# One tanh over two neighbouring sums: 16 instructions of 4096 columns in place of 32 of 2048

## The chip, the cores and the metric

The kernel runs on one core of a Trainium2 chip. The metric is the time of one execution on the device in microseconds (us). Its engines are TensorE (PE in the rows; PEld is its weight load), VectorE (DVE), ScalarE (ACT), GpSimd (POOL) and SyncE (SP), which here only issues transfers. They run their own instruction lists in order and wait for each other by semaphores.

## The reference

The reference is a small decoder of four layers on 16 batches of 64 tokens with 128 features. Each layer adds a kind of attention and a mixture of experts to `x`. The change touches only the attention of layer 2:

```python
def _L2_xattn_ref(features, masks, textual_features, q_masks, Ws, W, w, b, Wcw, bcw, Wcb, bcb):
    txt_proj = jnp.einsum('btd,de->bte', textual_features, Ws)
    feat_proj = jnp.einsum('bfd,de->bfe', features, W)
    h = jnp.tanh(txt_proj[:, None, :, :] + feat_proj[:, :, None, :] + b[None, None, :, :][..., 0, :])
    rho = jnp.einsum('bftd,d->bft', h, w[:, 0])
    qm = q_masks.astype(jnp.float32)
    rho = rho + (1.0 - qm)[:, None, :] * NEG
    att = jax.nn.softmax(rho, axis=-1)
    txt_h = jnp.einsum('bft,btd->bfd', att, textual_features)
    w_s = jnp.tanh(jnp.einsum('bfd,od->bfo', txt_h, Wcw) + bcw)
    b_s = jnp.tanh(jnp.einsum('bfd,od->bfo', txt_h, Wcb) + bcb)
    return w_s * features + b_s
```

For each batch, each of 64 feature rows is summed with each of 64 text rows, 128 values each; tanh of all of it, and a product with the vector `w`.

## The kernel before

Everything is kept with the 128 features on partitions and the 1024 tokens in the free dimension, in two halves `t` of 512. The stage before ends with a norm (`norm(4)`) and the next begins with `norm_rest(5)` and the experts of layer 2. Between them stands `pair_sums`, once for each engine, with each engine's work written out by hand in one loop over `g`.

The work is cut into 32 couples `g` of a batch `g // 2` and one half of its feature rows, 32 rows by 64 text rows, so 2048 columns each. Couple `g` goes through these steps:

- its sum, `work<-...`, is made by VectorE for even `g` (L1151, `sumA`) and by GpSimd for odd `g` (L1471, `sumB`), into buffer `g % 6` of `pairs`, which lies in `work`;
- its tanh is taken in place by ScalarE (L858), with the bias `l2b` from a tile;
- its dot with `w` is made by TensorE (L571) in four products of 512 columns, into one of two PSUM banks (couples 0 to 15, then 16 to 31). When it is done, the buffer is free for the sum of `g + 6`.

Other work stands in the same loops at fixed couples, and its place decides who waits for whom:

- TensorE projects keys for layer 3 ahead of the dots of 4 and 5 (L426, L427), which VectorE rotates at `g` 7 and 8, ahead of sum 8 (L1017 to L1019). Then TensorE projects values ahead of each dot of 8 to 15 (L436), two steps for each of four parts, and VectorE copies a part at `g` 11, 13, 15 and 17 (L1035), so ahead of sums 12, 14, 16 and 18.
- VectorE makes the softmax of the first 16 couples at `g` 20 (L1095 to L1097); ScalarE's exponential for it stands at `g` 19 (L836). The shares and the weighing stand at 22 and 24, and ScalarE's small tanh of the weights at `g` 25 (L841).
- TensorE spreads these weights ahead of the dots of 28 and 29 (L546), and VectorE updates the first half of `x` at `g` 30, ahead of sum 30 (L1123 to L1126). Ahead of the dot of 31 TensorE makes the mean of the next norm (L372).

Behind the loop follow the softmax and the update of the second half, and the next norm.

Of the kernel before, what the change touches and what calls it, by code (L numbers as in the profile page):

```python
# [21 lines left out]
ACT = mybir.ActivationFunctionType  # L22
# [59 lines left out]
def flamingo(nc, a, out):  # L82
    ctx = ExitStack()
    with ctx:
# [3 lines left out]
        def sem(name):  # L88
            return ctx.enter_context(nc.semaphore(name))
# [42 lines left out]
        l2pad, l2uvpad, l2b = packed["l2pad"], packed["l2uv"], packed["l2b"]  # L132
# [40 lines left out]
        pairs = work[:, 0:12 * T].rearrange("p (r c) -> p r c", r=6)  # L173
# [32 lines left out]
        x2 = {k: sem(f"x2_{k}") for k in ("feat", "fb", "sumA", "sumB", "tanh", "dot", "soft", "exp", "wb", "tw", "d", "bc")}  # L206
# [24 lines left out]
        def half(t):  # L231
            return slice(t * HALF, (t + 1) * HALF)
# [21 lines left out]
        POOL_SUMS = [g for g in range(2 * B) if g % 2]  # L254
# [106 lines left out]
        def _(pe):  # L361
            def keep_busy(count, bank):


                for _ in range(count):
                    pe.matmul(ps[:, bank], ident16, warm, start=True, stop=True)

            def norm_mean(j, t):

                if j:  # L370
                    pe.wait_ge(x_done[t], j)
                pe.matmul(ps[:, t], cen_w, x[:, half(t)], start=True, stop=True).then_inc(ln["mean"], 1)  # L372

            def norm_var(j, t):

                pe.wait_ge(ln["sq"], 2 * j + t + 1)
                for i in range(HT):
                    c = t * HT + i
                    mm = pe.matmul(ps[:, 2 + t, i:i + 1], sq[:, c * P:(c + 1) * P], var_w[:, :], start=True, stop=True)  # L379
                mm.then_inc(ln["var"], 1)  # L380

            def norm_spread(j, t):

                pe.wait_ge(ln["diag"], 2 * j + t + 1)
                pe.matmul(ps[:, 4 + t], ones_w[:, :], diag[:, half(t)], start=True, stop=True).then_inc(ln["bc"], 1)  # L385
# [37 lines left out]
            def prepare_keys(i, t):  # L423

                w, bank = (wqk1, wqk3)[i], KBANK[i][t]
                pe.matmul(ps[:, bank], w[:, 2], ctxT[:, half(t)], start=True, stop=True)  # L426
                pe.matmul(ps[:, bank + 1], w[:, 3], ctxT[:, half(t)], start=True, stop=True).then_inc(pre["proj"], 1)  # L427

            def prepare_values(i, q, part=None):

                w, r = (wqk1, wqk3)[i], 4 * i + q
                if q >= 2 and not part:
                    pe.wait_ge(pre["vcp"], r - 1)
                for b in range(4 * q + 2 * (part or 0), 4 * q + (2 if part == 0 else 4)):
                    for h2 in range(2):
                        mm = pe.matmul(ps[h2 * S:(h2 + 1) * S, VBANK[i] + q % 2, (b % 4) * P:(b % 4 + 1) * P],  # L436
                                       ctxT[:, b * S:(b + 1) * S], w[:, 4], start=True, stop=True)
                if part != 0:
                    mm.then_inc(pre["v"], 1)
# [103 lines left out]
            def weights_out(t, r):  # L543

                pe.wait_ge(x2["d"], 2 * t + r + 1)
                pe.matmul(ps[:, (0, 6)[t] + r], ones_w[:, :], (diag, sq)[r][:, half(t)], start=True, stop=True).then_inc(x2["bc"], 1)  # L546

            def pair_sums():

                pe.wait_ge(pre["txtcp"], 2)  # L550
                for t in range(2):
                    pe.wait_ge(ln["n"], 2 * 4 + t + 1)
                    pe.matmul(ps[:, FEAT[t]], l2w[:, 1], n[:, half(t)], start=True, stop=True).then_inc(x2["feat"], 1)
                for g in range(2 * B):

                    if g in (4, 5):
                        prepare_keys(1, g - 4)
                    if 8 <= g < 16:
                        if g == 8:
                            pe.wait_ge(pre["k"], 4)  # L560
                        prepare_values(1, (g - 8) // 2, g % 2)
                    if g == 28:
                        pe.wait_ge(pre["vcp"], 8)
                    if g in (28, 29):
                        weights_out(0, g - 28)
                    if g == 31:
                        norm_mean(5, 0)
                    pe.wait_ge(x2["tanh"], g + 1)
                    for q in range(4):

                        mm = pe.matmul(ps[32 * q:32 * q + 32, DOTS[g // B]], l2pad[:, 31 - g:63 - g],  # L571
                                       pairs[:, g % 6, q * 512:(q + 1) * 512], start=(g % B == 0), stop=(g % B == B - 1))
                    mm.then_inc(x2["dot"], 1)
                norm_var(5, 0)
                keep_busy(8, 3)
                norm_spread(5, 0)
                keep_busy(4, 3)
                for r in range(2):
                    weights_out(1, r)
# [142 lines left out]
            moe(MOES[1])  # L722
            norm(4, prepare_text)
            pair_sums()
            norm_rest(5)
            moe(MOES[2])
# [7 lines left out]
        def _(act):  # L734

            def norm_square(j, t):
                act.wait_ge(ln["mean"], 2 * j + t + 1)
                act.activation(sq[:, half(t)], ps[:, t], ACT.Square).then_inc(ln["sq"], 1)  # L738

            def norm_copy(j, t):  # L740
                act.copy(xc[:, half(t)], ps[:, t]).then_inc(ln["xc"], 1)
# [21 lines left out]
            def split_hi_up(m, e):  # L763

                s, u = mo[m.layer], e % m.slots
                if m.layer == 2:
                    act.wait_ge(w2_up_in[e % STAGE], 16 * (e // STAGE + 1))
                    if e >= 8:
                        act.wait_ge(s["hid"], 2 * (e - 7))
                    act.copy(up2(w_hi, e), up2_f32(e)).then_inc(s["whu"], 1)  # L770
                    return
                act.wait_ge(w_in[m.layer][u], 16 * (e // m.slots + 1))
                if e >= m.slots:
                    act.wait_ge(s["hid"], m.n * (e - m.slots + 1))
                o = u * m.width
                act.copy(w_hi[:, o:o + m.up], w_f32[:, o:o + m.up]).then_inc(s["whu"], 1)
# [57 lines left out]
            def softmax_exp(t):  # L834
                act.wait_ge(x2["soft"], t + 1)
                act.activation(ps[:, DOTS[t]], ps[:, DOTS[t]], ACT.Exp).then_inc(x2["exp"], 1)  # L836

            def weights_tanh(t):
                act.wait_ge(x2["wb"], t + 1)
                for r in range(2):  # L840
                    ins = act.activation(stp[:, 2 + r], stp[:, r], ACT.Tanh, bias=l2b[:, 1 + r:2 + r])  # L841
                ins.then_inc(x2["tw"], 1)

            def pair_sums():
                for t in range(2):
                    act.wait_ge(x2["feat"], t + 1)
                    act.copy(xc[:, half(t)], ps[:, FEAT[t]]).then_inc(x2["fb"], 1)
                for g in range(2 * B):
                    if g == 19:
                        softmax_exp(0)  # L850
                    if g == 25:
                        weights_tanh(0)
                    of_pool = len([p for p in POOL_SUMS if p <= g])
                    if g in POOL_SUMS:
                        act.wait_ge(x2["sumB"], of_pool)
                    else:
                        act.wait_ge(x2["sumA"], g + 1 - of_pool)
                    act.activation(pairs[:, g % 6], pairs[:, g % 6], ACT.Tanh, bias=l2b[:, 0:1]).then_inc(x2["tanh"], 1)  # L858
                norm_square(5, 0)
                norm_copy(5, 0)  # L860
                for e in range(STAGE, STAGE + 2):
                    split_hi_up(MOES[2], e)
                softmax_exp(1)
                for e in range(STAGE + 2, 8):
                    split_hi_up(MOES[2], e)
                weights_tanh(1)
# [92 lines left out]
            prepare_text()  # L959
            first_weights(MOES[2])  # L960
            pair_sums()
            norm_rest(5)
            moe(MOES[2])
# [636 lines left out]
```

## Time and profile before

| | |
|---|---|
| median of 3 runs | 670.05 us (666.01 to 670.86) |
| the profiled execution's own time | 664.23 us |
| its span, first to last instruction | 662.1 us |
| mean granted clock of TensorE | 0.969 of full speed |
| busy: PE, DVE, ACT, POOL | 582.9, 467.8, 393.9, 116.0 us |
| the stage of the change | about 313 to 388 us |

The rows further down are from the profiled execution, counted from its first instruction. Its own time is some 2 us more than its span, for what lies around it, and 5.8 us less than the median of the runs.

### The profile page before, as it was taken

The page shows a single profiled execution, that of the slowest core. Times are in us where ns is not written, and L with a number is a line of the kernel's source. Part 1 is how long each engine was busy: PE and PEld are TensorE (multiplying, and loading weights), DVE is VectorE, ACT ScalarE, POOL GpSimd, SP SyncE. Part 2 cuts the span into 40 slices and gives each one's busy share as a digit, 9 for nine tenths or more (in the row PEclk, how much of TensorE's full clock was granted, in tenths as well). Part 3 has the DMA queues.
Part 4 walks back from the last instruction along what each step waited for, and adds up shares of the span by engine and source line. Part 5 has one row for each costly group of instructions (what it writes and reads, how often), then busy time and mean ns, then how long its engine had stood idle before and what let it go on. Part 6 is the DMA issues. An engine that isn't in the chain of part 4 may idle for free.

```text
span 662.1 us, 8458 instructions
## 1 busy us (share of the span) xinstructions
PE 582.9 (88%) x3205; PEld 393.4 (59%) x3211; DVE 467.8 (71%) x672; ACT 393.9 (60%) x501; POOL 116.0 (18%) x66
## 2 busy tenths in 40 slices
PE   5889999888898999998775558899997988999997
PEld 3458888656656777774121124656643665888885
DVE  4876878686636889886689653846766755678785
ACT  4278888534635566555989743433204654888884
POOL 6530000040010000003999500003104000000000
PEclk9999999986998999999899979999999899999999
DMA  6207010120001712020000000163412000621200
GB/s 225 63 21 273 33 64 0 68 68 2 2 1 25 265 35 68 0 64 25 9 2 0 1 0 0 33 241 125 145 34 96 2 2 0 217 104 33 64 0 32
DMA packets 15483, 40.40 MB, mean 61 GB/s; under 512 B 2218, under 2 KB 6570, under 8 KB 15444
## 3 DMA queue, kind: packets, MB, share of 16 engines
q1 hardware_dynamic: 15444, 39.88, 17.5%
q8 instruction: 25, 0.41, 0.3%
q14 instruction: 14, 0.11, 0.1%
HBM read 39.17 MB, written 0.70 MB: 60 GB/s over the span
## 4 chain that ended last, share of the span: by engine, by line
PE 67%; DVE 14%; ACT 11%; issue 3%; DMA 2%; POOL 2%; DVEq 0%; SPq 0%; ACTq 0%
PE ps L594 41%; ACT work L858 7%; PE ps L631 3%; PE ps L480 3%; PE ps L505 2%; PE ps L492 2%; PE ps L385 2%; PE ps L372 2%; PE ps L379 2%; DMA w_f<-in_w 2%; PE ps L608 2%; PE ps L610 1%; PE ps L609 1%; PE ps L571 1%; DVE diag L981 1%
## 5 line engine op out<-in xcount | busy, mean ns | idle before, releaser
L1270 DVE TENSOR_TENSOR h_lo<-h_act,h_hi 128x1024 fp32r<-128x1024 f32 (+2 forms) x116 | 115.9, 999 | 46.8 <-ACT h_hi L900 46.8
L594 PE MATMUL ps<-n_hi,w_hi 128*128 128x512 f32 (+1 forms) x232 | 81.7, 400 | 4.6 <-DVE h_act L1247 2.4
L1444 POOL TENSOR_TENSOR rstd<-var_eps,minus_half 128x4 f32<-128x4 f32 x16 | 16.8, 1057 | 378.4 <-DVE var_eps L977 378.4
L900 ACT CAST h_hi<-h_act 128x1024 fp32r<-128x1024 f32 x68 | 71.4, 1050 | 18.1 <-PE ps L594 16.4
L594 PE MATMUL ps<-n_hi,w_lo 128*128 128x512 f32 (+1 forms) x232 | 80.3, 394 | 0.0
L594 PE MATMUL ps<-n_lo,w_hi 128*128 128x512 f32 (+1 forms) x232 | 80.2, 393 | 0.0
L594 PE MATMUL ps<-h_hi,w_hi 128*128 128x512 f32 (+1 forms) x184 | 61.8, 394 | 5.5 <-DVE h_lo L1270 5.5
L858 ACT ACTIVATE work<-work,p_rest 128x2048 f32<-128x2048 f32 x32 | 61.3, 1990 | 8.6 <-DVE work L1151 8.4
L594 PE MATMUL ps<-h_hi,w_lo 128*128 128x512 f32 (+1 forms) x184 | 61.2, 391 | 0.0
L594 PE MATMUL ps<-h_lo,w_hi 128*128 128x512 f32 (+1 forms) x184 | 61.1, 390 | 0.0
L571 PE MATMUL ps<-work,p_rest 128*32 128x512 f32 x256 | 36.0, 641 | 26.0 <-ACT work L858 26.0
L1471 POOL TENSOR_TENSOR work<-xc,txt 128x2048 f32<-128x2048 f32 x16 | 57.6, 3623 | 2.6 <-PE ps L571 1.9
L594 PEld LDWEIGHTS ps<-n_hi,w_hi 128*128 128x128 f32 (+1 forms) x232 | 42.5, 185 | 17.3 <-DVE h_act L1247 3.5
L892 ACT ACTIVATE h_act<-ps 128x512 f32<-128x512 f32 (+1 forms) x48 | 28.5, 597 | 40.1 <-PE ps L594 40.0
L594 PEld LDWEIGHTS ps<-n_lo,w_hi 128*128 128x128 f32 (+1 forms) x232 | 43.1, 186 | 10.6 <-issue 0.2
L594 PEld LDWEIGHTS ps<-n_hi,w_lo 128*128 128x128 f32 (+1 forms) x232 | 43.0, 185 | 10.5
L1247 DVE SCALAR_TENSOR_TENSOR h_act<-ps,h_act 128x512 f32<-128x512 f32 (+1 forms) x48 | 33.0, 687 | 16.7 <-ACT h_act L892 16.6
L594 PEld LDWEIGHTS ps<-h_hi,w_hi 128*128 128x128 f32 (+1 forms) x184 | 34.2, 188 | 15.8 <-DVE h_lo L1270 8.4
L738 ACT ACTIVATE sq<-ps 128x512 f32<-128x512 f32 x16 | 9.4, 595 | 53.2 <-PE ps L372 53.2
L885 ACT ACTIVATE h_act<-ps 128x1024 f32<-128x1024 f32 x36 | 36.9, 1025 | 4.8 <-PE ps L594 4.8
L594 PEld LDWEIGHTS ps<-h_hi,w_lo 128*128 128x128 f32 (+1 forms) x184 | 34.5, 188 | 7.5
L594 PEld LDWEIGHTS ps<-h_lo,w_hi 128*128 128x128 f32 (+1 forms) x184 | 34.6, 188 | 7.3
(221 smaller groups left out, 1063.2 us busy)
## 6 DMA issues: line engine op xcount, KB each, us to landing
work<-g_rows SPq DMA_DIRECT2D x38, 512.0 KB, 7.1
w_f<-in_w SPq DMA_DIRECT2D x17, 512.0 KB, 3.4
w_f<-in_w SPq DMA_DIRECT2D x8, 544.0 KB, 3.6
w_f<-in_w SPq DMA_DIRECT2D x16, 128.0 KB, 2.2
w_f<-in_w SPq DMA_DIRECT2D x16, 64.0 KB, 2.3
p_rest<-in_p_rest SPq DMA_DIRECT2D x1, 714.0 KB, 8.2
p_attn<-in_p_attn SPq DMA_DIRECT2D x1, 546.5 KB, 6.9
x<-in_xT SPq DMA_DIRECT2D x1, 512.0 KB, 3.5
```

The costliest lines, as they stand in the source:

```text
L480: mm = pe.matmul(ps[b * S:(b + 1) * S, SCB[p % 2] + top, cols], q_rows[rows, low, c:c + S], kexp[rows, 2 * p + b], start=True, stop=True)
L571: mm = pe.matmul(ps[32 * q:32 * q + 32, DOTS[g // B]], l2pad[:, 31 - g:63 - g], pairs[:, g % 6, q * 512:(q + 1) * 512], start=(g % B == 0) ...
L594: mm = pe.matmul(dst[i], wap(wt, e, lo, size, rows), mv[i], start=(first and c == 0), stop=(last and c == 2))
L631: pe.matmul(ps[:, acc + k], down2(e), h_part[step % 16], start=False, stop=(e == m.experts - 1)).then_inc(s["h_used"], 1)
L858: act.activation(pairs[:, g % 6], pairs[:, g % 6], ACT.Tanh, bias=l2b[:, 0:1]).then_inc(x2["tanh"], 1)
L885: act.activation(h_act[:, sl], ps[:, 2 * sl:2 * sl + 2].rearrange("p a c -> p (a c)"), ACT.Gelu, **kw).then_inc(s["act"], 1)
L892: act.activation(h_part[step % parts][0:size], ps[0:size, 2 * sl], ACT.Silu, **kw).then_inc(s["act"], 1)
L900: act.copy(h_hi[:, sl], h_act[:, sl]).then_inc(s["hi"], 1)
L1247: dve.scalar_tensor_tensor(h, ps[0:size, 2 * sl + 1], b3, h, ALU.add, ALU.mult).then_inc(s["mul"], 1)
L1270: dve.tensor_tensor(h_lo[at_slot], src, h_hi[at_slot].bitcast(F32), ALU.subtract).then_inc(s["lo"], 1)
L1444: pool.tensor_tensor(rstd[:, r], var_eps[:, r], minus_half[:, r], ALU.pow).then_inc(ln["rstd"], 1)
L1471: pool.tensor_tensor(*sum_of(g, xc[:, half(g // B)]), ALU.add).then_inc(x2["sumB"], 1)
```

## The change

ScalarE takes the tanh of couples `g - 1` and `g` in one instruction at every odd `g`. The two buffers are neighbours in `pairs`, so the instruction runs over 4096 columns without a gap. It waits for both sums, that of VectorE and that of GpSimd. The semaphore `tanh` counts 16 instead of 32, and TensorE waits for `g // 2 + 1` ahead of the dot of `g`. The exponential at `g` 19 and the small tanh at `g` 25 keep their places in the text, so they stand ahead of the tanh of (18,19) and (24,25) and no longer between their halves. Sums, dots and all other steps stay as they are.

```diff
@@ -565,7 +565,7 @@
                     if g == 31:
                         norm_mean(5, 0)
-                    pe.wait_ge(x2["tanh"], g + 1)
+                    pe.wait_ge(x2["tanh"], g // 2 + 1)
                     for q in range(4):
@@ -850,12 +850,11 @@
                     if g == 25:
                         weights_tanh(0)
-                    of_pool = len([p for p in POOL_SUMS if p <= g])
-                    if g in POOL_SUMS:
-                        act.wait_ge(x2["sumB"], of_pool)
-                    else:
-                        act.wait_ge(x2["sumA"], g + 1 - of_pool)
-                    act.activation(pairs[:, g % 6], pairs[:, g % 6], ACT.Tanh, bias=l2b[:, 0:1]).then_inc(x2["tanh"], 1)
+                    if g % 2:
+                        act.wait_ge(x2["sumA"], g // 2 + 1)
+                        act.wait_ge(x2["sumB"], g // 2 + 1)
+                        both = pairs[:, g % 6 - 1:g % 6 + 1].rearrange("p r c -> p (r c)")
+                        act.activation(both, both, ACT.Tanh, bias=l2b[:, 0:1]).then_inc(x2["tanh"], 1)
```

## Rows read from the trace of the kernel before

**Rows 1.** The page's costliest groups: the tanh and GpSimd's sums

```profile
L858 ACT ACTIVATE work<-work,p_rest 128x2048 f32<-128x2048 f32 x32 | 61.3, 1990 | 8.6 <-DVE work L1151 8.4
...
L1471 POOL TENSOR_TENSOR work<-xc,txt 128x2048 f32<-128x2048 f32 x16 | 57.6, 3623 | 2.6 <-PE ps L571 1.9
```

**Rows 2.** List of waits, 313 to 388 us: total, times, longest

```profile
ACT work L858 <- DVE work L1151: 8.4, 3, 4.2
```

**Rows 3.** The chain that ended last, in order of time: start, us, what

```profile
323.36 1.07 PE ps L571 x8
...
326.33 1.00 PE ps L571 x8
...
333.54 20.93 ACT work L858 x11
```

**Rows 4.** Timeline at the stage's start: start, us, engine, line

```profile
313.86 36.00 POOL L1471 TENSOR_TENSOR work<-xc,txt 128x2048 f32<-128x2048 f32 x10 [0.60 <-ACT xc L847]
...
317.41 1.93 PE L571 MATMUL ps<-work,p_rest 128*32 128x512 f32 x8 [4.25 <-ACT work L858]
317.51 13.36 ACT L858 ACTIVATE work<-work,p_rest 128x2048 f32<-128x2048 f32 x7 [0.16 <-POOL work L1471]
```

**Rows 5.** Groups of instructions of ScalarE, shapes kept apart

```profile
L885 ACT ACTIVATE h_act<-ps,p_attn 128x1024 f32<-128x1024 f32 x32 | 35.7, 1115 | 4.2 <-PE ps L594 4.1
...
L892 ACT ACTIVATE y_g<-ps,p_rest 128x512 f32<-128x512 f32 x8 | 5.5, 688 | 9.5 <-PE ps L610 9.5
```

**Rows 6.** Timeline from the dot of 5 to sum 12

```profile
329.18 2.82 PE L571 MATMUL ps<-work,p_rest 128*32 128x512 f32 x24
...
335.59 1.06 PE L571 MATMUL ps<-work,p_rest 128*32 128x512 f32 x8 [3.01 <-ACT work L858]
...
336.59 0.66 PE L436 MATMUL ps<-p_rest,ctxT 128*64 128x128 f32 x8
...
337.29 0.86 DVE L1035 COPY vblk<-ps 64x256 f32<-64x256 f32 x2 [1.59 <-PE ps L436]
...
338.19 2.29 DVE L1151 TENSOR_TENSOR work<-ps,txt 128x2048 f32<-128x2048 f32 x1
```

**Rows 7.** Timeline of the first softmax and of sums 24 and 26

```profile
351.75 0.69 DVE L1095 TENSOR_TENSOR ps<-ps,mbias 128x512 f32<-128x512 f32 x1
...
353.19 0.70 DVE L1097 TENSOR_TENSOR ps<-ps,st 128x512 f32<-128x512 f32 x1
...
354.38 0.58 ACT L836 ACTIVATE ps<-ps 128x512 f32<-128x512 f32 x1
...
354.89 11.57 ACT L858 ACTIVATE work<-work,p_rest 128x2048 f32<-128x2048 f32 x6
...
362.15 4.48 DVE L1151 TENSOR_TENSOR work<-ps,txt 128x2048 f32<-128x2048 f32 x2
```

**Rows 8.** Timeline from the dot of 28 to tanh 30

```profile
374.55 1.06 PE L571 MATMUL ps<-work,p_rest 128*32 128x512 f32 x8
...
375.55 1.12 PE L546 MATMUL ps<-sq,ones_w 128*128 128x512 f32 x2
...
380.43 3.89 ACT L858 ACTIVATE work<-work,p_rest 128x2048 f32<-128x2048 f32 x2 [4.20 <-DVE work L1151]
```

**Rows 9.** Timeline of the last two dots and the mean between them

```profile
382.48 1.93 PE L571 MATMUL ps<-work,p_rest 128*32 128x512 f32 x8 [4.81 <-ACT work L858]
...
384.35 1.67 PE L372 MATMUL ps<-x,p_first 128*128 128x512 f32 x2
...
385.94 1.07 PE L571 MATMUL ps<-work,p_rest 128*32 128x512 f32 x8
```

**Rows 10.** Windows: busy us of each engine, then TensorE's granted clock, DMA share, GB/s

```profile
331.00:336.00 5.00, 1.99 (x24) 0.66 (x24) 4.70 (x3) 2.46 (x2) 5.00 (x3) 1.00 0.01 2
...
318.00:321.00 3.00, 2.77 (x16) 0.20 (x8) 3.00 (x2) 3.00 (x2) 3.00 (x1) 0.56 0.00 0
382.00:385.00 3.00, 2.52 (x9) 0.70 (x10) 0.00 (x0) 2.32 (x2) 0.00 (x0) 0.51 0.00 0
```

## The prediction

> **What bounds the kernel now.** The change touches one stage, the pair sums of layer 2, from 313 to 388 us of a span of 662. I read the page first for the costliest groups: 32 tanh instructions keep ScalarE busy for 61.3 us, 16 sums keep GpSimd busy for 57.6 us [rows 1]. Busy time alone says that ScalarE fills the stage. The list of waits then says where it doesn't: ScalarE stands for 8.4 us in three places, each time for a sum made by VectorE [rows 2]. Last I took the chain of waits through the stage, which shows what those sums in turn waited for. The reader should see there two kinds of stretch. In the long ones the tanh itself is the chain, 11 of them in 20.93 us. Between them the chain leaves ScalarE and goes through TensorE and VectorE: from the dot of couple 3 (323.36) over the two key projections and the dot of couple 4, which stand in TensorE's order between dots, and over the rotation of the keys on VectorE, to sum 8 and tanh 8 at 333.54 [rows 3]. The pace of the tanh counts in the first kind. In the second kind the latency from a tanh to its own dot counts, and this latency is what the change lengthens.
>
> **The pace: what is gained.** Seven tanh in a row take 13.36 us [rows 4], so one follows the other after (13.36 - 1.99) / 6 = 1.89 us, 3.79 us for a couple of them. For the double size no row exists. Two activations with a bias from a tile, of 512 and 1024 elements, take 688 and 1115 ns [rows 5], 0.83 ns per element. That puts 2048 more elements at 1.71 us: an instruction of 3.70 us, and a pitch of 1.89 + 1.71 = 3.60 us. The upper end is two whole ones, 3.98 us, if nothing fixed is shared; I take 3.70, since three sizes lie on one line. The gain is 0.19 us for each of 16 couples, 3.0 us at most, where ScalarE is the chain. GpSimd makes one sum per couple; ten sums take 36.00 us, also 3.60 us each [rows 4], so it just keeps that pace and gives no cover beyond it.
>
> The Trainium skill, "ScalarE: Activation LUTs", section "What ACT_TABLE_LOAD costs", gives about 280 ns plus 0.833 ns per element for an activation with such a bias, and an overlap of about 93 ns between neighbours. By it the new one would be an estimated 3.69 us long and the saving 3.0 us; the rows at 512 and 2048 elements agree with it. Read as a rule for the whole stage it speaks for this change, with the result of the first rival below.
>
> **The latency: what is lost.** The first dot of a couple now waits for the end of the doubled tanh, so it starts a half instruction later relative to the sums. Where only ScalarE is next, six buffers hide this: 3.60 us of the next tanh cover a dot or two of about 0.94 us (three in 2.82 us [rows 6]) and a GpSimd sum. Where a step of TensorE between two dots feeds VectorE, it isn't hidden. I follow the chain with starts of tanh instructions; "before" stands in brackets.
>
> Step A, the keys. GpSimd's sum 1 ends at 317.49, so tanh (0,1) starts at 317.5, where tanh 1 started. Tanh (2,3) ends at 317.51 + 3.60 + 3.70 = 324.81, the dot of 2 starts at 324.87, and that of 3 at 325.80 (323.36). Tanh (4,5) ends at 328.41, before TensorE reaches the dot of 4 at 328.8, so all else in the chain of [rows 3] moves unchanged: 333.54 - 323.36 = 10.18 us later, at 335.98 (333.54), tanh (8,9) starts. Loss 2.4 us.
>
> Step B, the value copies. Tanh (8,9) ends at 339.68, and only then the dot of 8 runs. The projection of values stands in TensorE's order between the dots of 8 and 9; VectorE copies its result ahead of sum 12. From the start of dot 8 (335.59) to the end of sum 12 (338.19 + 2.29 = 340.48) it took 4.89 us, with 0.04 to the next step [rows 6]. Before, tanh 12 started at 341.11 and this was covered by 0.6 us. Now it isn't: 339.73 + 4.93 = 344.66 for tanh (12,13), while ScalarE is free at 335.98 + 7.20 = 343.18. A new wait of 1.5 us.
>
> Step C, the same again. Tanh (12,13) ends at 348.36; the dot of 12, values, copy and sum 16 give 348.41 + 4.93 = 353.34 for tanh (16,17) (348.70, four pitches of 1.89 after 341.11). ScalarE is free at 351.86, so another 1.5 us.
>
> Step D, the softmax. The exponential stood between tanh 18 and tanh 19, now it stands ahead of both, and they are queued behind its wait. Tanh (14,15) starts at 344.66 + 3.60 = 348.26 and ends at 351.96. The dot of 14, the values and the copy let sum 18 start at 354.6 and end at 356.8. The softmax on VectorE took 351.75 to 353.19 + 0.70 = 353.89, so 2.14 us [rows 7], and now ends at 358.95. The exponential starts at 359.0, and tanh (18,19) 0.51 us behind it (354.89 - 354.38 [rows 7]) at 359.5, ending at 363.2 (tanh 19: 354.89 + 1.99 = 356.88). Loss to here 6.3 us, of which 2.1 is ScalarE's wait.
>
> Step E, the gain. Four tanh follow at the pitch of 3.60. The weighing on VectorE ends about 367.5 and sum 24 about 369.7, against a need at 370.3, so no wait is added; the small tanh of the weights costs 0.3 as before. Before, sum 24 was ready just in time (the first of two sums that take 4.48 us from 362.15 [rows 7], with tanh 24 at 354.89 + 5 x 1.89 = 364.34). Tanh (26,27) ends at 377.9, and (28,29) at 381.5.
>
> Step F, the update. The second spread of weights stands behind the dot of 28. From that dot (374.55) over the spread (375.55) and three steps of VectorE with sum 30 to tanh 30 (380.43) it took 5.88 us [rows 8]. Dot 28 now waits for the end of tanh (28,29) and starts at 381.55, so tanh (30,31) starts at 387.43 and ends at 391.13 (tanh 31: 380.43 + 3.89 = 384.32). ScalarE's wait grows from 4.2 to 6.0 us. Loss to here 6.8 us.
>
> Step G, the tail. The dot of 30 ran under tanh 31 at 382.48, then the mean of the next norm and the dot of 31, to 385.94 + 1.07 = 387.01 [rows 9]: 4.53 us after tanh 30's end. All three now come behind the doubled tanh: 391.18 + 4.53 = 395.7. Loss 8.7 us. Behind this stage nothing is changed; its work is a chain of TensorE, VectorE and ScalarE, and starts that much later.
>
> Step H, TensorE's clock. Its records show 0.56 and 0.51 (mostly half, 1.2 GHz in place of 2.4) for the stretches behind idle times of 4.3 and 4.8 us, and 1.00 behind 3.0 us [rows 6, 10]; a dot behind the long ones took 1.93 [rows 4, 9] instead of 1.07 us. Three dots and a projection of values that ended at 332.0 and 332.6 (2.82 us from 329.18 [rows 6], and 0.66) move by 2.4, so ahead of the dot of 8 TensorE will now be idle from about 335.0 to 339.7, which is like the long ones. I add 1.0 us in step B (0.86 for the dot, the rest for the values); the low end is 0, the high end some 3 if the half clock lasts through B and C. The idle time ahead of the dot of 18, 4.2 us, isn't on the chain.
>
> Sum: A 2.4, B to D 3.9, E with F 0.5 (6.8 - 6.3), G 1.9, H 1.0: 9.7 us. No DMA is moved. The profiled execution took 664.23 us and would take 673.9. The median of the runs shown, 670.05, lies 5.8 us above it, and the runs themselves spread from 666.01 to 670.86; I put the sum on the median: 679.8 us.
>
> **The rivals.** First, the pace decides: the gain of 3.0 us comes through, because the dots of a couple go fast and the three places of VectorE have more room than I give them. 667 us. For it speaks ScalarE's busy share in the stage; against it that ScalarE already waits for VectorE three times, and that cover in B was 0.6 us only. It would need tanh (12,13) to start without a wait and the two new half instructions at the ends not to count; it decides only if A and G, 4.3 us by rows, are wrong too. Chance 0.05. By the Trainium skill's fixed cost per activation alone the result is this one.
>
> Second, the loss at the ends only: A (2.4), the growth of the wait in F (1.8) and G (1.9) stand, but B, C and D are absorbed, since sums run ahead in spare buffers, and the pace gives 2 to 3 us back. That is +3 to +4, 673.5 us, within 1%. For it: the chain is built from one execution, and VectorE is idle at times between 336 and 350. Chance 0.15.
>
> Third, more than I say: the half clock holds through B and C or comes back at the dots of 16 to 19 (+2 to +3), or the doubled instruction costs 3.98 us, on 12 couples of the chain 0.28 us each (+3.4). 683 us. For it: TensorE gets its dots in twos, so its idle times become fewer and longer everywhere. Chance 0.12. That the change doesn't do what it says, with one instruction running as two, is the last case of this rival.
>
> **How the numbers follow.** My forecast, about +7 to +12 us, has 0.68. Within 1% (6.7 us, about what a measurement of this kernel can tell) lie the second rival, nearly all of the first and the low edge of the forecast: 0.20. Faster by over 1% needs a gain of 6.7 us, more than the 3.0 that the pace can give, so only the spread of runs could show it: 0.02. Slower 0.78. The range goes from 671.5 (second rival, with a low run) to 684.5 (third rival).
>
> **What the profile would show.** Sixteen instructions on 128x4096 of 3.70 us (A, E); waits of ScalarE for VectorE at five or six places instead of three, in all some 15 us, with new ones at tanh (12,13) and (16,17) of 1.5 us or more, and one for the exponential's input of about 2; the last dot 4.5 us behind the last tanh; half clock at the dot of 8. I'm wrong if ScalarE waits three times again, if the new instruction isn't near 3.7 us, or if the time from 313 to the last dot isn't some 83 us (387.0 - 313.2 = 73.8 before).

## The result, and the profile after

The changed kernel takes 677.85 us (median of 4 runs, 677.64 to 678.40) where the kernel before takes 670.45 (4 runs, 666.01 to 672.30): a ratio of 1.0135, with a 95% interval of 1.0084 to 1.0186. Run once more on another occasion it gave 677.89 against 671.60, 1.0110 (1.0059 to 1.0161). Some runs of a kernel are slow as a whole; the ratios leave them out, the medians count them. By the medians it is slower by 7.4 and 6.3 us; the forecast was 9.7 more, 679.8. Its profiled execution took 678.03 us with a span of 676.1, 14.0 us over the span of before.

The page's costliest groups show the two things that were meant to happen: sixteen instructions instead of 32, and 58.6 us of ScalarE instead of 61.3 [rows 1]. The idle time in front of them doubled, from 8.6 to 17.7 us, and GpSimd, which hardly waited before (2.6), now waits 12.9.

```profile
L857 ACT ACTIVATE work<-work,p_rest 128x4096 f32<-128x4096 f32 x16 | 58.6, 3705 | 17.7 <-DVE work L1150 17.3
...
L1470 POOL TENSOR_TENSOR work<-xc,txt 128x2048 f32<-128x2048 f32 x16 | 57.6, 3621 | 12.9 <-PE ps L571 12.3
```

The list of waits from 313 to 400 us: ScalarE waits for VectorE's sums six times instead of three, 17.3 us instead of 8.4 [rows 2], the first of these 3.79 us at the start of the stage.

```profile
ACT work L857 <- DVE work L1150: 17.3, 6, 5.9
POOL work L1470 <- PE ps L571: 12.3, 6, 5.0
```

The chain of waits through the stage, to be held against [rows 3]. Before, 11 tanh stood in it in one piece. Now it leaves ScalarE behind most couples and goes down through dots, values, copies and a sum. Shown are the start, the stretch from (8,9) to sum 14, and the tail:

```profile
316.91 3.72 ACT work L857
...
320.67 5.68 PE ps L571 x32
...
335.47 3.72 ACT work L857
...
339.24 1.94 PE ps L571 x8
341.17 1.05 PE ps L436 x8
342.22 1.87 PE ps L571 x8
344.09 1.05 PE ps L436 x8
...
347.66 2.30 DVE work L1150
...
393.06 1.94 PE ps L571 x8
395.00 1.73 PE ps L372 x2
396.73 1.04 PE ps L571 x8
```

ScalarE's timeline in the changed kernel, with its idle time in brackets. The first row is the copy of the second half of the features, from which I count the stage, because no change reaches ahead of it; the following ones are the new waits ahead of (12,13), (14,15), (16,17) and the exponential, and the grown one of step F [rows 8]:

```profile
312.53 0.59 ACT L847 COPY xc<-ps 128x512 f32<-128x512 f32 x1 [0.27 <-PE ps L553]
...
345.49 3.71 ACT L857 ACTIVATE work<-work,p_rest 128x4096 f32<-128x4096 f32 x1 [2.70 <-DVE work L1150]
349.99 3.71 ACT L857 ACTIVATE work<-work,p_rest 128x4096 f32<-128x4096 f32 x1 [0.79 <-DVE work L1150]
354.17 3.71 ACT L857 ACTIVATE work<-work,p_rest 128x4096 f32<-128x4096 f32 x1 [0.47 <-DVE work L1150]
360.73 0.58 ACT L836 ACTIVATE ps<-ps 128x512 f32<-128x512 f32 x1 [2.85 <-DVE ps L1096]
...
389.30 3.71 ACT L857 ACTIVATE work<-work,p_rest 128x4096 f32<-128x4096 f32 x1 [5.93 <-DVE work L1150]
```

TensorE's timeline has the dot of 28, 5.88 us ahead of that last tanh:

```profile
383.42 1.06 PE L571 MATMUL ps<-work,p_rest 128*32 128x512 f32 x8 [0.62 <-ACT work L857]
```

Windows of the changed kernel; the third number from the right is TensorE's granted clock. Three more stretches besides the start lie near 0.5 [rows 10]:

```profile
338.00:345.00 7.00, 5.76 (x32) 1.85 (x32) 2.69 (x3) 4.78 (x2) 2.28 (x2) 0.52 0.00 0
362.00:369.00 7.00, 4.02 (x20) 0.80 (x24) 6.79 (x10) 7.00 (x3) 1.98 (x2) 0.51 0.00 0
389.00:396.00 7.00, 2.94 (x10) 0.70 (x10) 0.27 (x1) 3.71 (x1) 0.00 (x0) 0.54 0.00 0
```

From that copy to the end of the last dot of the stage, the profile before has 387.01 - 313.20 = 73.8 us and the one after has 396.66 + 1.06 - 312.53 = 85.2. Behind the last dot follow 275.1 and 278.4 us. So 11.4 us of the 14.0 lie in the stage. That is more than the 7.4 us between the medians, and the experiments had to show first why.

### The profile page after: what moved, and what is told of

Its sections match the earlier page's. It is cut to its first block, busy times and chain, and to the rows that moved or that the text cites. A ratio compares the mean times of both kernels' runs of the same rounds, so it can differ in the third digit from the quotient of the medians.

```text
span 676.1 us, 8458 instructions
## 1 busy us (share of the span) xinstructions
PE 590.4 (87%) x3205; PEld 397.5 (59%) x3211; DVE 468.2 (69%) x672; ACT 392.5 (58%) x485; POOL 116.0 (17%) x66
## 4 chain that ended last, share of the span: by engine, by line
PE 71%; DVE 14%; ACT 10%; issue 2%; POOL 2%; DMA 1%; DVEq 0%; SPq 0%; ACTq 0%
PE ps L594 40%; ACT work L857 5%; PE ps L631 4%; PE ps L480 3%; PE ps L492 2%; PE ps L571 2%; PE ps L505 2%; PE ps L385 2%; PE ps L608 2%; PE ps L372 2%; PE ps L610 2%; PE ps L609 2%; PE ps L379 1%; DVE diag L980 1%; DVE work L1150 1%
## 5 line engine op out<-in xcount | busy, mean ns | idle before, releaser
L857 ACT ACTIVATE work<-work,p_rest 128x4096 f32<-128x4096 f32 x16 | 58.6, 3705 | 17.7 <-DVE work L1150 17.3
L571 PE MATMUL ps<-work,p_rest 128*32 128x512 f32 x256 | 38.3, 707 | 34.2 <-ACT work L857 34.2
L594 PE MATMUL ps<-h_hi,w_lo 128*128 128x512 f32 (+1 forms) x184 | 61.3, 392 | 0.0
L1470 POOL TENSOR_TENSOR work<-xc,txt 128x2048 f32<-128x2048 f32 x16 | 57.6, 3621 | 12.9 <-PE ps L571 12.3
L571 PEld LDWEIGHTS ps<-work,p_rest 128*32 128x32 f32 x256 | 6.6, 120 | 57.9 <-ACT work L857 46.8
L1150 DVE TENSOR_TENSOR work<-ps,txt 128x2048 f32<-128x2048 f32 x16 | 36.2, 2286 | 4.9 <-PE ps L571 3.6
```

Of the source, the lines that this page charges most:

```text
L594: mm = pe.matmul(dst[i], wap(wt, e, lo, size, rows), mv[i], start=(first and c == 0), stop=(last and c == 2))
L857: act.activation(both, both, ACT.Tanh, bias=l2b[:, 0:1]).then_inc(x2["tanh"], 1)
L1150: dve.tensor_tensor(*sum_of(g, ps[:, FEAT[g // B]]), ALU.add).then_inc(x2["sumA"], 1)
L1470: pool.tensor_tensor(*sum_of(g, xc[:, half(g // B)]), ALU.add).then_inc(x2["sumB"], 1)
```

## The experiments

"Stage" is always the time from the copy of the second half of the features to the end of the last dot, "behind" the rest of the span. The ratios are to the kernel before as it ran on the same occasion. The median and the ratio come from all rounds of a kernel, stage and behind from one profiled execution, which can lie some us off its median.

| run | median us | ratio (95%) | stage | behind |
|---|---|---|---|---|
| before, first profile | 670.45 | | 73.8 | 275.1 |
| before, again | 671.28 | 0.9987 (0.9927 to 1.0046) | 77.6 | 280.1 |
| changed, again | 677.89 | 1.0110 (1.0059 to 1.0161) | 85.0 | 278.5 |
| joint wait, two instructions | 682.77 | 1.0168 (1.0137 to 1.0199) | 87.6 | 280.3 |
| first 16 doubled | 673.21 | 1.0040 (1.0010 to 1.0070) | 81.5 | 278.6 |
| last 16 doubled | 672.38 | 1.0018 (0.9995 to 1.0042) | 81.5 | 278.5 |
| moved, doubled | 667.21 | 0.9957 (0.9922 to 0.9991) | 75.8 | 277.5 |
| moved, single | 662.88 | 0.9896 (0.9863 to 0.9929) | 71.4 | 279.7 |
| changed, idle products | 675.06 | 1.0085 (1.0048 to 1.0121) | 83.6 | 277.6 |
| changed, values moved | 675.15 | 1.0082 (1.0052 to 1.0113) | 80.8 | 277.5 |
| changed, end single | 682.11 | 1.0186 (1.0148 to 1.0225) | 83.9 | 284.1 |
| changed, exponential moved | 677.32 | 1.0120 (1.0084 to 1.0156) | 84.5 | 280.1 |
| moved, single, idle products | 663.52 | 0.9915 (0.9884 to 0.9945) | 70.8 | 280.2 |

**The kernel before, profiled again.** No edit.

> The kernel before, unchanged, profiled once more. Its times spread from 663 to 673 us, and its first profile lies at the low end (span 662.1). If that profile was one of favourable clock phases, a second one shows half clock in the stage at other places, a wait of ScalarE ahead of tanh 8 of some 3.5 us instead of 2.66 (as in the run with the last 16 doubled, whose first half is the same code), and a stage some 2 to 3 us longer than 73.8; else the same stage within 0.5 us.

Its median is 671.28, but its span is 667.9 where the first profile had 662.1, with a mean clock of 0.940 instead of 0.969. ScalarE's timeline:

```profile
310.19 0.59 ACT L847 COPY xc<-ps 128x512 f32<-128x512 f32 x1 [0.27 <-PE ps L553]
...
331.40 7.68 ACT L858 ACTIVATE work<-work,p_rest 128x2048 f32<-128x2048 f32 x4 [3.52 <-DVE work L1151]
339.71 3.90 ACT L858 ACTIVATE work<-work,p_rest 128x2048 f32<-128x2048 f32 x2 [0.63 <-DVE work L1151]
...
380.49 3.89 ACT L858 ACTIVATE work<-work,p_rest 128x2048 f32<-128x2048 f32 x2 [4.93 <-DVE work L1151]
```

TensorE's timeline has the last dot of the stage, from whose end the stage is counted:

```profile
386.41 1.33 PE L571 MATMUL ps<-work,p_rest 128*32 128x512 f32 x8
```

The wait ahead of tanh 8 is 3.52 us, as expected, two small ones ahead of tanh 12 and 14 are new, and the one ahead of tanh 30 is 4.93 instead of 4.20: it is the same program with more of TensorE's work at half clock (the dots of 26 and 27 took 3.69 us together, and 1.07 and 1.06 in the first profile). The stage is 77.6 us, 3.8 more than in the first profile and not 2 to 3. Twenty-nine runs of the kernel before on that occasion lie between 662.3 and 674.7, 23 of them over 669: the first profile (664.23) was one of the low ones. The changed kernel's stage of 85.0 to 85.2 is 7.5 us longer than this one, which fits the 6.3 to 7.4 us between the medians. The kernel with the last 16 doubled, below, is in its first half the same program, and its waits there are those of this profile (3.51, 0.63 and 0.59 us).

**Latency against pace: wait for both, but two instructions.**

```diff
-                        both = pairs[:, g % 6 - 1:g % 6 + 1].rearrange("p r c -> p (r c)")
-                        act.activation(both, both, ACT.Tanh, bias=l2b[:, 0:1]).then_inc(x2["tanh"], 1)
+                        act.activation(pairs[:, g % 6 - 1], pairs[:, g % 6 - 1], ACT.Tanh, bias=l2b[:, 0:1])
+                        act.activation(pairs[:, g % 6], pairs[:, g % 6], ACT.Tanh, bias=l2b[:, 0:1]).then_inc(x2["tanh"], 1)
```

> ScalarE waits for both sums as in the changed kernel, but takes two tanh of 2048 columns, and only the second signals. So the latency is that of the changed kernel and the pace that of the kernel before: a couple takes 1.89 + 1.99 = 3.88 us instead of 3.71, with a pitch of 3.79 instead of 3.60. If the loss is latency (my theory), this is slower than the changed kernel by 0.19 us for each of the 10 to 12 couples on the chain, some 2 us: 680 us, and the stage from the first tanh to the last dot about 83 us. If the doubled instruction itself were dear (rival: it blocks something or runs longer than two), this would be faster than the changed kernel, near 672.

682.77 us, 4.9 over the changed kernel, where 2 were expected. In the profiles 2.5 us lie in the stage (87.6 against 85.1) and 1.8 behind it. The chain at its end, the last two dots and the mean between them, mostly at half clock:

```profile
394.46 1.93 PE ps L571 x8
396.39 2.01 PE ps L372 x2
398.40 1.57 PE ps L571 x8
```

The last tanh ends 82.0 us after the copy, in the changed kernel 80.5 (393.01 - 312.53). So the doubled instruction is not what is dear: it repays 1.5 us up to there, and the other 1.0 us came in the tail, most of it from half clock in the mean and the last dot, which took 1.73 and 1.04 us in the changed kernel. The joint wait and the joint signal cost 9 to 10 us: 87.6 against 77.6, less that stretch of clock. The rival, that the instruction itself is dear, would have given 672.

**Half of the couples doubled.** With `DOUBLED` the couples whose tanh is taken together, `g < B` in one kernel and `g > B` in the other, and TensorE's wait counted accordingly:

```diff
+        DOUBLED = [g for g in range(1, 2 * B, 2) if g < B]
...
-                    pe.wait_ge(x2["tanh"], g // 2 + 1)
+                    pe.wait_ge(x2["tanh"], tanhs(g))
```

> Doubled tanh for couples 0 to 15 only; 16 to 31 are single again. Latency theory: steps A, B, C and the half clock stay, so ScalarE still waits ahead of (8,9) and (12,13); D loses its wait for the exponential in part, F and G are as in the kernel before (waits 4.2 us, last dot 2.7 us behind the last tanh). About +6 us over the kernel before, 676 us. A pace theory gives a gain of 8 x 0.19 = 1.5 us, 669.

> Doubled tanh for couples 16 to 31 only. Latency theory: A, B, C are gone (first half as in the kernel before), ScalarE waits some 1.4 us for the exponential, F costs +1.8 and G +1.9, the pace gives 1.1 back: +4 us, 674 us. The losses of this and of the run with the first 16 add up to that of the changed kernel within 2 us. A pace theory gives -1.5 us.

Both medians came out lower than expected (673.21 for 676, 672.38 for 674), and their losses, 2.1 and 1.3 us, don't add up to 6 or 7. The stages do: 81.5 and 81.5 are each 3.9 over 77.6, together 7.8, against 7.5 for both at once. Part of what is missing in the medians may lie behind the stage, where no instruction differs and both took 1.5 us less than the second profile of before; one profile for each does not settle it, and that of the last 16 is an execution of 674.49 us, 2.1 over its median. By the ratios the first half of the change loses by itself (1.0010 to 1.0070), while for the last half the interval reaches down to 0.9995, and only the stage shows its loss.

In the last half the wait ahead of (30,31) grew more than the 1.8 us that were expected:

```profile
385.38 3.71 ACT L867 ACTIVATE work<-work,p_rest 128x4096 f32<-128x4096 f32 x1 [7.37 <-DVE work L1160]
```

The dots of 26 and 27 took 3.64 us there, at half clock, and only behind them came the dot of 28, at 379.50, again 5.88 us ahead of the tanh.

**What stands between two dots, moved to the borders of couples.** In the changed kernel:

```diff
-                    if g in (4, 5):
-                        prepare_keys(1, g - 4)
+                    if g == 4:
+                        prepare_keys(1, 0)
+                        prepare_keys(1, 1)
...
-                        prepare_values(1, (g - 8) // 2, g % 2)
+                        if g % 2 == 0:
+                            prepare_values(1, (g - 8) // 2, 0)
+                            prepare_values(1, (g - 8) // 2, 1)
...
-                    if g in (28, 29):
-                        weights_out(0, g - 28)
-                    if g == 31:
+                    if g == 28:
+                        weights_out(0, 0)
+                        weights_out(0, 1)
+                    if g == 30:
                         norm_mean(5, 0)
...
-                    if g == 19:
+                    if g == 20:
                         softmax_exp(0)
```

> All tanh doubled as in the changed kernel, but what stood between the two dots of a couple on TensorE stands ahead of both now: both key projections ahead of dot 4, both steps of a part of the values ahead of dots 8, 10, 12, 14, both spreads ahead of dot 28, the mean ahead of dot 30; the exponential stands behind tanh (18,19). Latency theory: B, C, D vanish, A shrinks to about 1.4 us, F is 4.3 us of waiting as before, G is gone; the pace gives up to 3 us. About 669 us, 9 us under the changed kernel. If the places between the dots don't matter (rival: the loss comes from the buffers coming free later, or from the clock alone), it stays near 677.

667.21 us, 10.7 under the changed kernel as it ran on the other occasion: with all tanh still doubled, the loss is gone. ScalarE's timeline:

```profile
312.06 0.59 ACT L851 COPY xc<-ps 128x512 f32<-128x512 f32 x1 [0.27 <-PE ps L553]
...
333.94 10.91 ACT L861 ACTIVATE work<-work,p_rest 128x4096 f32<-128x4096 f32 x3 [2.56 <-DVE work L1154]
345.57 10.91 ACT L861 ACTIVATE work<-work,p_rest 128x4096 f32<-128x4096 f32 x3 [0.72 <-DVE work L1154]
...
380.43 3.71 ACT L861 ACTIVATE work<-work,p_rest 128x4096 f32<-128x4096 f32 x1 [4.05 <-DVE work L1154]
```

TensorE's timeline has the last two dots in one row, at half clock:

```profile
384.20 3.64 PE L575 MATMUL ps<-work,p_rest 128*32 128x512 f32 x16 [4.61 <-ACT work L861]
```

The wait ahead of (8,9) is 2.56 instead of 3.62. (12,13) starts without one, where it was 2.70; 0.72 is left ahead of (14,15). The exponential no longer waits, (24,25) now waits 1.01 us, and the wait ahead of (30,31) is 4.05 instead of 5.93.

**The same moves with 32 single tanh.** The edit for TensorE is the same, the tanh are those of the kernel before, the exponential stays at `g` 19.

> The steps of TensorE moved to the borders of couples as in the run with all doubled and moved, but with 32 single tanh. Latency theory: without the latencies between dots the doubling only saves the fixed cost, so this should be slower than the doubled and moved one by 1 to 3 us: 668 to 670. If this is faster than the doubled and moved one (rival: doubling still costs at the first tanh and at the last), 664 to 666.

My expectation of 668 to 670 was wrong, and the rival's right: 662.88 us, 4.3 under the doubled one, and 1.0% faster than the kernel before. ScalarE's timeline:

```profile
310.54 0.59 ACT L851 COPY xc<-ps 128x512 f32<-128x512 f32 x1 [0.27 <-PE ps L553]
...
330.79 20.93 ACT L862 ACTIVATE work<-work,p_rest 128x2048 f32<-128x2048 f32 x11 [2.58 <-DVE work L1155]
...
376.36 3.90 ACT L862 ACTIVATE work<-work,p_rest 128x2048 f32<-128x2048 f32 x2 [3.00 <-DVE work L1155]
```

TensorE's, with the dots of 30 and 31:

```profile
378.42 1.07 PE L575 MATMUL ps<-work,p_rest 128*32 128x512 f32 x8 [2.88 <-ACT work L862]
380.31 1.63 PE L575 MATMUL ps<-work,p_rest 128*32 128x512 f32 x8 [0.83 <-ACT work L862]
```

Tanh 8 starts 330.79 - 310.54 = 20.3 us after the copy, (8,9) of the doubled kernel at 333.94 - 312.06 = 21.9. Tanh 30 starts after 65.8 us, (30,31) after 68.4. From there to the end of the last dot pass 5.6 against 7.4 us, since the dot of 30 runs while tanh 31 does. These are 1.6, 0.9 and 1.8 us, the 4.4 us between the stages. Some of the 1.8 is clock: the two last dots took 3.64 us in the doubled kernel and 1.07 and 1.63 in this one. Even with nothing between the dots, a doubled tanh delays its first dot and the keys, the update and the tail wait for dots. The gain in pace, 0.19 us for a couple, shows where the tanh follow each other and doesn't make up for it.

How much of the 1.0% comes from shorter waits is open. Against the second profile of the kernel before the stage is 6.2 us shorter, against the first only 2.4, and the fastest runs of the kernel before, from 662.3 us, are as fast as this one. No run separates shorter waits from a half clock that falls less often on the chain.

**One step at a time in the changed kernel.** Values only (the `prepare_values` part of the edit above), end only (`DOUBLED` with `g < 28`), exponential only (`g == 20`).

> The changed kernel; alone moved are the two steps of a part of the values, now both ahead of dots 8, 10, 12 and 14. If steps B and C are what I say, the copies on VectorE no longer wait for the doubled tanh: ScalarE's waits ahead of (12,13), (14,15) and (16,17), 2.70, 0.79 and 0.47 us in the profile of the changed kernel, shrink to under 1 us together, and so does part of the loss in D: -3 to -4 us, 674 us. If they are cover for something else, 677.9.

ScalarE's timeline, with tanh (14,15) to (16,17) in one row and the exponential below it:

```profile
308.78 0.59 ACT L849 COPY xc<-ps 128x512 f32<-128x512 f32 x1 [0.27 <-PE ps L553]
...
343.33 7.31 ACT L859 ACTIVATE work<-work,p_rest 128x4096 f32<-128x4096 f32 x2 [0.41 <-DVE work L1152]
351.57 0.58 ACT L838 ACTIVATE ps<-ps 128x512 f32<-128x512 f32 x1 [0.93 <-DVE ps L1098]
```

675.15 us, 2.7 less by the medians, just short of the expected 3 to 4; the stage of the profiled execution is 4.3 us shorter, but that execution took 669.33 us, the lowest of twelve. The waits are as steps B, C and part of D say: those ahead of the couples 12 to 17, 3.96 us together, are down to 0.41, and the exponential's from 2.85 to 0.93. (30,31) starts 71.2 us after the copy instead of 76.8; the tail then took 9.6 us instead of 8.4, with the last dot at 1.94 us.

> The changed kernel with single tanh for couples 28 to 31. Steps F and G undone: wait ahead of tanh 30 back from 5.93 to about 4.2 us, the last dot 2.7 to 3.5 instead of 4.7 us behind the last tanh: -3.5 us, 674.4 us. If the ends don't count, 677.9.

This missed: 682.11 us instead of 674.4. The timeline of the end:

```profile
377.75 1.92 PE L575 MATMUL ps<-work,p_rest 128*32 128x512 f32 x16 [1.68 <-ACT work L867]
...
379.50 1.99 ACT L862 ACTIVATE work<-work,p_rest 128x2048 f32<-128x2048 f32 x1
...
380.66 1.06 PE L575 MATMUL ps<-work,p_rest 128*32 128x512 f32 x8
...
386.54 2.00 ACT L859 ACTIVATE work<-work,p_rest 128x2048 f32<-128x2048 f32 x1 [5.06 <-DVE work L1160]
...
392.46 1.93 PE L575 MATMUL ps<-work,p_rest 128*32 128x512 f32 x8
```

Tanh 28 ends early, at 379.58, but its dot starts at 380.66: the dots of 26 and 27 both stand behind the doubled tanh (26,27) and run from 377.75, and the first spread of weights comes after them. TensorE's list is late, not the tanh, so the wait ahead of tanh 30 only falls from 5.93 to 5.06. The 4.2 us that I expected came from the first profile, too: in the second one the wait is 4.93 with 32 single tanh. And the tail stays at half clock to the end, the last dot at 1.93 us. The stage wins 1.2 us instead of 3.5. Most of the rest of the miss lies behind the stage, 284.1 us for the 278.4 of the changed kernel, with the same instructions there. Windows of this kernel and of the changed one in the experts of layer 2, with the granted clock third from the right, first this one:

```profile
445.00:466.00 21.00, 21.00 (x36) 10.37 (x35) 6.83 (x11) 2.35 (x4) 0.00 (x0) 0.51 0.60 215
```

and the changed one:

```profile
447.00:455.00 8.00, 8.00 (x14) 3.54 (x13) 3.12 (x5) 0.69 (x1) 0.00 (x0) 0.57 0.86 344
```

Twenty-one us at half clock (0.51) with TensorE busy all the time, against about eight. All six runs of this kernel lie between 680.46 and 683.50, so this is no single mishap. Why the half clock holds there so long I did not test.

> The changed kernel with the exponential of the first softmax behind tanh (18,19) instead of ahead of it. Step D: ScalarE's wait of 2.86 us for the softmax goes, sum 18 is then last with 0.7 us, and the later shares may cost 0.6 us ahead of (24,25): -1.5 to -2 us, 676 us. A rival is that the wait only moves on: 677.9.

677.32 us, 0.6 less, and 0.6 us less of stage: the exponential's wait is gone, but (18,19) now waits 0.79 us for sum 18 and (24,25) 0.85 us for sum 24. VectorE makes that sum no earlier than in the changed kernel: its row starts 56.4 us after the copy in both. What is left of the 2.85 us is 1.2: (30,31) starts after 75.6 instead of 76.8 us, and the tail, with the mean at 2.08 us, takes half of it back. So more than half of the wait moved on, as the rival says, and the expected 1.5 to 2 us did not come.

**TensorE kept busy.** In the changed kernel 30, 16, 18 and 24 idle products ahead of the dots of 0, 8, 18 and 30; in the moved single one 16, 6 and 10 ahead of 0, 8 and 30:

```diff
+                    if g in {0: 30, 8: 16, 18: 18, 30: 24}:
+                        keep_busy({0: 30, 8: 16, 18: 18, 30: 24}[g], 4)
                     pe.wait_ge(x2["tanh"], g // 2 + 1)
```

> The changed kernel with idle products on TensorE (30 ahead of dot 0, 16 ahead of dot 8, 18 ahead of dot 18, 24 ahead of dot 30, into a bank that nobody reads), so that it doesn't fall to half clock there. My step H and the clock in the tail: dots of 8 and 30 take 1.07 instead of 1.94 us, the wait ahead of (12,13) shrinks by 1 to 1.5 us, the tail by 1.6: 673 to 675 us. If the clock plays no part, 677.5.

The chain of waits, with (8,9), the dot of 8, (12,13), the dots of 26 and 27, and the dot of 30:

```profile
332.92 3.72 ACT work L859
...
336.68 1.07 PE ps L573 x8
...
341.59 3.72 ACT work L859
...
375.98 3.64 PE ps L573 x16
...
390.57 1.06 PE ps L573 x8
```

675.06 us, 2.8 less, at the far end of the expectation. At the padded places the dots of 8 and 30 take 1.07 and 1.06 us instead of 1.94, and (12,13) starts 8.7 us behind (8,9) instead of 10.0. Counted from the copy (310.13), (8,9), (12,13) and (14,15) start after 22.8, 31.5 and 35.1 us: that is the forecast to 0.1 us, if the 1.0 us of step H is left out. But half clock came at other places: at the projection of values behind the dot of 12 and at the dot of 13 (1.12 and 1.94 us; (16,17), which hangs on that projection and to which ScalarE now comes earlier, waits 2.01 us instead of 0.47), and behind tanh (26,27), 3.64 us for two dots that took 1.92 before, and the wait ahead of (30,31) grew from 5.9 to 7.3. So (30,31) starts 76.7 us after the copy, hardly before the 76.8 of the changed kernel, and the 1.5 us that the stage is shorter all come in the tail.

> Single tanh, TensorE's steps at the borders of couples, and idle products ahead of dots 0 (16), 8 (6) and 30 (10). In the profile without them the three dots 0 to 2 took 5.72 us at half clock and stand in the chain, and the last dots 1.6 us. If the clock is all that is left at these places: -2 to -3 us, 660 us. If half clock only moves to another stretch, 663.

663.52 us against 662.88: no gain in the time. The stage is 0.6 us shorter, 0.5 us more lie behind it, and there the mean clock is 0.95 in both. The three dots of the expectation are those of 1 to 3. With the idle products the first two took 1.06 us each, but then had to wait for their tanh, and the dot of 3 fell to half clock (1.93 us); the key projections behind it start 12.0 us after the copy in both kernels. So half clock moved, and where it was gone the dots had been waiting anyway.

## Why the prediction was right

The sign and the mechanism held, and the size by a balance of two errors: the doubled tanh delays the first dot of each couple, and where a step between two dots feeds VectorE, ScalarE waits for it. The joint wait with two instructions shows that it is latency and not the instruction; the moved steps show that it is this latency. By step, as starts after the copy of the features (forecast from 313.20, with 1.0 for step H from (12,13) on):

| | forecast | measured |
|---|---|---|
| doubled tanh | 3.70 us | 3.71 |
| A: (8,9) starts | 22.8 | 22.9 |
| B: (12,13) | 32.5 | 33.0 |
| (14,15) | 36.1 | 37.5 |
| C: (16,17) | 41.1 | 41.6 |
| D: (18,19) | 47.3 | 48.7 |
| F: (30,31) | 75.2 | 76.8 |
| G: end of the last dot | 83.5 | 85.2 |

**Pace.** By rows 3.60 us; three doubled tanh in 10.91 us are (10.91 - 3.71) / 2 = 3.60. The Trainium skill ("ScalarE: Activation LUTs", "What ACT_TABLE_LOAD costs") gave an estimate of 3.69 us for one, and the trace agrees with 3.71. As a rule for the whole it fails, since the first rival (667 us), a gain of 3 us, did not come.

**A, B, C, F.** Three waits stand where they were put, with 3.6 us ahead of (8,9), 2.7 ahead of (12,13), 5.9 ahead of (30,31). The fourth, 1.5 us ahead of (16,17), came in two parts, 0.79 us ahead of (14,15) and 0.47 ahead of (16,17); from (12,13) to (16,17) it is 8.68 us as in step C. Moving the values alone removed B and C, which shows those two. For F the chain from the dot of 28 to (30,31) took 5.88 us (389.30 - 383.42), the figure of the prediction. Its removal was shown only as part of the moves together; undoing the end alone showed that its cause includes the couple (26,27), which step F had started from and did not list as a cause.

**D.** The wait is there, 2.85 us for the forecast 2.1. To move the exponential alone made (30,31) start 1.2 us earlier and the time 0.6 us shorter; to move the values alone took 1.9 us off this wait. So the place of the exponential is the smaller part of it: the softmax is late mainly because the dots are.

**H is the term that was mis-sized.** I gave 1.0 us for half clock at the dot of 8. It lasted over two dots and two projections of values (339.24 to 345.1). It cost 1.5 us at (12,13) and 2.4 at (14,15), whose sum waits for the second copy of values; I had (14,15) follow at the pace. At (16,17) only 0.5 us more than forecast is left, since that one hangs on the dot of 12; but sum 18 hangs on the dot of 14, and from D on the stage is 1.4 to 1.7 us later than forecast. The kernel with idle products shows it: with the dot of 8 at full clock (12,13) and (14,15) start where the forecast without H has them.

**The base was off the other way.** I put the sum, 9.7 us, on the median. The profile I summed against had a stage of 73.8 us, while a second profile of the same kernel has 77.6. The stage grew by 11.4 us over the first, by 7.5 over the second. So the two errors partly cancelled, which was luck: a stage 1.7 us longer than forecast, and a base 3.8 us better than that of the second profile. I had seen that the profile lay 5.8 us under the median and still took its waits for the usual ones: in the second profile tanh 8 starts after 21.2 us instead of 20.3, tanh 30 after 70.3 instead of 67.2, so part of what A to F charge to the change is in the kernel before as a rule. The second rival (loss at the ends only, 673.5) falls, since B and C are there; of the third only the longer half clock was real, as the instruction took 3.71 and not 3.98 us.

## What to carry to other kernels

An instruction made twice as long saves one fixed cost, here 0.19 us, and makes its first consumer wait half an instruction longer, here 1.8 us. Before merging, look in the consumer's list for work that stands between the two halves and that something else waits for; move it to the border of the pair or leave the pair apart. In this kernel the moves alone, without merging, won 1.0%, in part perhaps by the clock. And compare stages with two profiles of the kernel before, not one: here they differed by 3.8 us, half of the effect.

## What the runs showed of the hardware

The same list of instructions behind the stage took 275.1 to 284.1 us in these profiles, and the more of it was granted 1.2 instead of 2.4 GHz, the longer it took. The mean granted clock from the last dot to the end was 0.98 of full speed where it took 275.1 us (first profile of the kernel before), 0.96 at 278.4 (changed kernel), 0.95 at 280.1 (second profile) and 0.94 at 284.1 (end single). The longest stretch at half clock, 21 us, fell on TensorE busy all the time. Twelve runs of the moved single kernel spread over 5.0 us, twenty-nine of the kernel before over 12.3.

Where idle products stood ahead of a dot it ran at full clock, 1.07 instead of 1.94 us, and half clock then appeared elsewhere, as in the 3.64 us of the dots of 26 and 27. That those places follow from the idle products was not tested.
